# VectorE's dependent chains stood in pieces between the one-hot compares of a graph network's first aggregation

## The reference, cut to what matters

```
h = relu(layernorm(x))
norm = deg_inv[src] * deg_inv[dst]
m = norm * (h[dst] + (h[dst] * h[src]) @ W1.T + b)         # layer 0
x = x + leaky_relu(segment_sum(m, dst))
h = relu(layernorm(x))
h = relu(h @ Ws0.T + mean(h[src], dst) @ Wn0.T + c0)        # layer 1, two SAGE steps
h =      h @ Ws1.T + mean(h[src], dst) @ Wn1.T + c1
out = x + h
```

## Time and profile before

| | us |
|---|---|
| median of 3 runs | 3341.88 |
| lowest and highest | 3338.53, 3342.33 |
| profiled execution, its own time | 3346.14 |
| its span, first to last instruction | 3344.1 |
| aggregation 0 in it, slots 1 to 55 and the last products | 265 to about 1616 |

### The profile page before, as it was taken

One profiled execution on the slowest core, in us unless ns is written; L12 is line 12 of the kernel. 1 busy time (PEld: TensorE's weight loads), 2 busy tenths in 40 slices (PEclk: granted clock), 3 DMA queues, 4 the chain that ended last, 5 costly groups with the idle time before them and its releaser, 6 DMA issues.

```text
span 3344.1 us, 73461 instructions
## 1 busy us (share of the span) xinstructions
PE 2979.4 (89%) x27729; PEld 2602.2 (78%) x27729; DVE 1935.4 (58%) x5525; ACT 1322.4 (40%) x3331; POOL 2237.0 (67%) x2220
## 2 busy tenths in 40 slices
PE   1068788899998898989899999999999999999998
PEld 0046577688787787878788888888888888888888
DVE  6689999999898898989354444432221221222221
ACT  1324566687787787878244444421110000000000
POOL 7716765677777777777366665666664777677673
PEclk9999999999999999999999999999999999999999
DMA  7362344455455455545566666676665666666664
GB/s 213 96 123 79 105 121 120 125 152 158 140 164 151 139 151 164 158 138 150 160 202 221 219 196 212 219 238 195 215 201 166 215 221 219 209 209 211 215 216 153
DMA packets 479015, 581.78 MB, mean 174 GB/s; under 512 B 62620, under 2 KB 443265, under 8 KB 478169
## 3 DMA queue, kind: packets, MB, share of 16 engines
q1 hardware_dynamic: 352132, 404.43, 37.6%
q0 software_dynamic: 69168, 145.24, 16.6%
q10 hardware_dynamic: 57360, 27.34, 3.0%
HBM read 412.81 MB, written 164.77 MB: 173 GB/s over the span
## 4 chain that ended last, share of the span: by engine, by line
PE 59%; POOL 17%; DVE 16%; issue 7%; DMA 1%; ACT 1%; ACTq 0%; DVEq 0%; POOLq 0%
PE ps L1670 48%; POOL arena L1445 13%; DVE arena L1975 6%; DVE arena L1970 5%; PE ps L1581 4%; PE ps L1640 4%; POOL arena L1414 3%; PE ps L1616 2%; DMA arena<-parts,arena 1%; DVE arena L1989 1%; PE ps L1606 0%; POOL arena L1422 0%; DVE arena L2042 0%; DVE arena L2076 0%; DVE arena L2082 0%
## 5 line engine op out<-in xcount | busy, mean ns | idle before, releaser
L1445 POOL DMA_INDIRECT arena<-parts,arena x1991 | 2058.5, 1034 | 836.0 <-issue 573.1
L1670 PE MATMUL ps<-arena 128*128 128x256 f16 (+2 forms) x18816 | 2469.1, 274 | 65.1 <-DVEq L2043 58.0
L1670 PEld LDWEIGHTS ps<-arena 128*128 128x128 fp8e3 x18816 | 1805.2, 98 | 285.1 <-ACT arena L1237 59.6
L1237 ACT ACTIVATE arena<-ps 128x392 fp8e3<-128x392 f32 x2176 | 1048.9, 500 | 630.5 <-PE ps L1640 588.2
L1640 PE MATMUL ps<-arena 128*128 128x196 bf16 (+1 forms) x5806 | 786.7, 241 | 76.2 <-DVE arena L1975 66.5
L1640 PEld LDWEIGHTS ps<-arena 128*128 128x128 bf16 x5806 | 500.3, 101 | 189.5 <-DVE arena L1975 78.7
L1975 DVE TENSOR_TENSOR arena<-arena 128x1176 bf16<-128x1176 bf16 (+6 forms) x1016 | 644.7, 635 | 0.0
L1989 DVE TENSOR_TENSOR arena<-arena 128x256 bf16<-128x256 bf16 x864 | 232.7, 314 | 700.0 <-PE ps L1581 696.3
L1970 DVE TENSOR_TENSOR arena<-arena 128x768 bf16<-128x768 bf16 (+5 forms) x1016 | 539.8, 531 | 105.7 <-PE ps L1640 91.1
L1581 PE MATMUL ps<-arena 128*128 128x256 f16 (+1 forms) x1991 | 291.8, 275 | 39.4 <-DMA arena<-parts,arena 38.9
L2058 DVE SCALAR_TENSOR_TENSOR arena<-ps,rdegs,arena 128x128 f32<-128x128 f32 x196 | 68.6, 350 | 382.5 <-PE ps L1670 350.7
(11 more groups left out here) (192 smaller groups left out, 1142.1 us busy)
## 6 DMA issues: line engine op xcount, KB each, us to landing
arena<-counts SPq DMA_DIRECT2D x132, 1568.0 KB
counts<-arena SPq DMA_DIRECT2D x68, 1568.0 KB
arena<-parts,arena POOLq DMA_INDIRECT x1991
arena<-table SPq DMA_DIRECT2D x294, 64.0 KB
arena<-parts SPq DMA_DIRECT2D x28, 448.0 KB, 5.0
parts<-arena ACTq DMA_DIRECT2D x108, 64.0 KB
table<-arena ACTq DMA_DIRECT2D x108, 64.0 KB
parts<-arena SPq DMA_DIRECT2D x14, 455.0 KB, 9.5
```

Of the source, the lines that this page charges most:

```text
L1237: act.activation(to, ps[:, unit_bank(q), 0:(b - a) * tiles].rearrange("p (n a) -> p a n", n=b - a), ACT.Copy, saturate=False).then_inc(s_e ...
L1445: pool.indirect_dma_start(to, None, parts_of[nth], bass.IndirectOffsetOnAxis(ap=tail_idx[:, i, first + c:first + c + 1], axis=0)).then_inc ...
L1670: m = pe.matmul(bank(b, 0, w), stage[k][:, a, :], rows_in[nth][:, a, 0:w], start=e == 0, stop=e == tiles - 1, skip_group_check=True)
```

## The change

It touches aggregation 0 alone, on VectorE, and two places of small work on TensorE and ScalarE. `one_hots` is cut into `low_one_hots` and `high_one_hots`. `take` (for aggregation 0) is cut into `take_sum` and `take_rest`, `settle` into six functions of one instruction each, and `finish` into two. The loop issues one piece in front of a buffer's low compare and one between its low and high compare. A chain that started before buffer f is spread over f, f+1 and f+2. A piece waits for the last one by a semaphore as before (`link` only notes the value), but a compare stands between the two.

The sum of a dense tile (`take_sum`) is issued between the compares of the buffer before, so one high compare sooner, and `s_free` is raised by its second instruction itself. The check against the degree is now made last, from the copied sum in SBUF (130 columns are copied, not 129). `settle` begins at 0.20 and 0.58 of a slot and not at 0.22 and 0.66. TensorE's `w1_product` moves from product 60 to product 50, and ScalarE's two `turned_u` from 42 and 88 to 27 and 66 per cent of the slot.

```diff
-                take_before.setdefault(during(starts_at[g] + 1 if e else in_slot(s, 0.85)), []).append(2 * s + e)
-                settle_before.setdefault(during(in_slot(g, 0.66 if e else 0.22)), []).append(2 * s + e)
+                settle_before.setdefault(during(in_slot(g, 0.58 if e else 0.2)), []).append(2 * s + e)
+            tail_before.setdefault(during(in_slot(s, 0.85)), []).append(2 * s)
+            dense_before.setdefault(during(starts_at[g] + 1), []).append(2 * s + 1)
...
-                        now = [round(len(here) * part / 100) for part in (0, 8, 42, 46, 50, 54, 60, 88, 92, 96)]
+                        now = [round(len(here) * part / 100) for part in (0, 8, 27, 46, 50, 54, 60, 66, 92, 96)]
...
-                    if e == 60:
+                    if e == 50:
                         w1_product(nth, 2 * s)
...
+            def take_sum(j):
...
+                of = sums[:, r % SUMS, 0:width]
+                then(dve.tensor_scalar(of, bank(b, ONE, ONE + width), 1.0 / HIGH, None, ALU.mult))
+                dve.tensor_tensor(of[:, 0:ONE], bank(b, 0, ONE), of[:, 0:ONE], ALU.add).then_inc(free, 1)
+
+            def take_rest(j):
...
+                dve.tensor_tensor(u[:, e, :], tin[:, r % DEEP, :], of[:, 0:P], ALU.mult).then_inc(s_u, 1)
+                dve.tensor_tensor(s0b[:, t:t + 1], of[:, P:ONE], dinv[:, t:t + 1], ALU.mult)
+                if t < GROUPS:
+                    dve.scalar_tensor_tensor(agrees[:, t:t + 1], of[:, ONE:ONE + 1], HIGH, degree[:, t:t + 1], ALU.mult, ALU.is_equal)
...
+            def link(ins):
+
+                chain[0] += 1
+                ins.then_inc(s_chain, 1)
+                return chain[0]
...
+            def settle_leaky(j):
...
+                dve.wait_ge(s_chain, settled[0])
+                settled[0] = link(dve.scalar_tensor_tensor(v, v, SLOPE, v, ALU.mult, ALU.max))
...
+                    for j in dense_before.get(f, []):
+                        take_rest(j)
+                    for j in tail_before.get(f, []):
+                        take_sum(j)
                     for n in ready_before.get(f, []):
                         ready(0, n)
                     for j in settle_before.get(f, []):
-                        settle(j)
+                        settle_sum(j)
+                    for j in settle_before.get(f - 1, []):
+                        settle_leaky(j)
+                    for j in settle_before.get(f - 2, []):
+                        settle_stats(j)
                     for j in finish_before.get(f, []):
-                        finish(j)
+                        finish_root(j)
+                    low_one_hots(f)
+                    for j in tail_before.get(f, []):
+                        take_rest(j)
+                    for j in dense_before.get(f + 1, []):
+                        take_sum(j)
+                    for j in settle_before.get(f, []):
+                        settle_self(j)
+                    for j in settle_before.get(f - 1, []):
+                        settle_row(j)
+                    for j in settle_before.get(f - 2, []):
+                        settle_mean(j)
+                    for j in finish_before.get(f, []):
+                        finish_shift(j)
                         split_tile(0, j)
-                    one_hots(f)
+                    high_one_hots(f)
```

More of the change, by code:

```diff
@@ L2082, in settle, with settle_stats, settle_mean, finish_root @@
                 dve.scalar_tensor_tensor(x1[:, r % 3, :], v, 1.0 / (HIGH * BOTH), xin[:, r % DEEP, :], ALU.mult, ALU.add).then_inc(s_x1, 1)
+            def settle_stats(j):
+                r = at(0, j - 4)
+                if r is None:
+                    return
                 dve.wait_ge(s_x1, r + 1)
+                averaged[0] = link(dve.bn_stats(stats[:, r % 2, :], x1[:, r % 3, :]))
+            def settle_mean(j):
+                r = at(0, j - 4)
+                if r is None:
+                    return
+                dve.wait_ge(s_chain, averaged[0])
                 if r >= 2:
                     dve.wait_ge(s_std, r - 1)
-                then(dve.bn_stats(stats[:, e, :], x1[:, r % 3, :]))
-                dve.bn_aggr(tile_mv[:, e, :], stats[:, e, :]).then_inc(s_var, 1)
-            def finish(j):
+                dve.bn_aggr(tile_mv[:, r % 2, :], stats[:, r % 2, :]).then_inc(s_var, 1)
+            def finish_root(j):
                 r = at(0, j - 5)
@@ L2097, in finish, with finish_shift @@
                     dve.wait_ge(s_h, r - 1)
-                then(dve.reciprocal(tile_rstd[:, e:e + 1], tile_std[:, e:e + 1]))
+                rooted[0] = link(dve.reciprocal(tile_rstd[:, e:e + 1], tile_std[:, e:e + 1]))
+            def finish_shift(j):
+                r = at(0, j - 5)
+                if r is None:
+                    return
+                e = r % 2
+                dve.wait_ge(s_chain, rooted[0])
                 dve.scalar_tensor_tensor(tile_shift[:, e:e + 1], tile_mv[:, e, 0:1], -1.0, tile_rstd[:, e:e + 1], ALU.mult, ALU.mult).then_inc(s_shift, 1)
@@ L2142, in _ @@
                             dve.tensor_scalar(rdegs[:, k, :], rdeg[:, :], norms[:, 12 + k:13 + k], None, ALU.mult)
-                    for j in take_before.get(f, []):
-                        take(0, j)
+                    for j in dense_before.get(f, []):
+                        take_rest(j)
+                    for j in tail_before.get(f, []):
+                        take_sum(j)
                     for n in ready_before.get(f, []):
```

124 lines of the change are left out of this document (79 added, 45 removed).

## The result

| | us |
|---|---|
| before, median of 4 runs | 3341.8 (3338.5 to 3342.3) |
| after, median of 4 runs | 3382.2 (3380.8 to 3382.6) |
| ratio | 1.0122, 95% interval 1.0105 to 1.0140 |
| profiled execution after, its span | 3380.4 |

I had forecast 3314 us, in a range of 3290 to 3338. The change is slower, outside the range and on the other side.

What follows compares the result with a forecast made beforehand. VectorE was taken to bound 341 to 674 us and GpSimd's gathers 692 to 1568; links 22, `s_free` 3 and the later stretch 3 saved 28 us of 3346.1: 3318, or 3314 on the median's scale, range 3290 to 3338.

Steps and rivals of the forecast that it cites:

- the gathers' own duration: GpSimd's 597 gathers, 692 to 1568 us: lengthened by the compare running at their start; taken as 0, ends -22 and +31 us.
- The formula from the evenly spread starts: Mean gather excess if starts spread evenly over VectorE's compares, each costing up to its length less 0.13 us: 0.141 us; measured 0.178.
- One of my own signs of being wrong: The forecast is wrong if the mean gather differs from 1119 ns by more than 30 ns.
- The links: VectorE's chains before 674 us: seven links a tile lose their waits and overlap; 22 us, between 11.3 and 23.1.
- `s_free`: Signal to TensorE before 674 us comes about 0.9 us sooner, shortening its waits; 3 us, bounds 0 and 4.6.
- Granted clock above 0.97 in the first part: Sign in the changed profile: TensorE's granted clock above 0.97 from 341 to 674 us.
- Waits for one-hots and `s_free`: TensorE before 674 us: `s_free` waits near 0.8 us each or gone; growing one-hot waits would make the forecast wrong.
- The tie at 674 us: TensorE ends GpSimd's last long wait, 17.9 us, at 674, so VectorE's earlier savings move the whole rest forward.
- Gathers fall into step: Rival: each gather starts at a compare's beginning; decides from 47 ns a gather; at 80 ns 3362 us; chance 0.08.
- Links cost nothing: Rival: VectorE's pipe drain makes freed links worth nothing, leaving 3 + 3 us; 3336 us, chance 0.07.
- the Trainium skill's port rule: VectorE instructions with two SBUF inputs hold up GpSimd's SBUF reads; pieces count alike before and after, so no time.

Runs made afterwards that it cites:

- filled: joined with an unused, independent two-SBUF-input instruction between `settle_self` and `settle_leaky`, filling the idle moment; 3374.6 us, ratio 1.0103.
- joined: The change with `settle_leaky` moved right behind `settle_self`, so that it waits for its input again; 3312.5 us, ratio 0.9915.
- gapped: The change in its own order, but `settle_leaky` waits for the end of the high compare ahead of it; 3359.4 us, ratio 1.0049.
- the two light kernels: The kernel before and the change, each gathering at most 3 of up to 5 chunks a subgroup in aggregation 0; 3311.2 and 3262.2 us.
- after_again: The change, run again unaltered against the kernel before; 3382.9 us against 3342.5, ratio 1.0124.
- the ten orders: The kernel before, the change and eight follow-up kernels that rearrange sums, chain links, waits or added instructions, all gathers kept; 3312.5 to 3382.2 us.
- openings: The change with a one-column reciprocal ahead of three pieces of the `settle` chain; 3364.0 us, ratio 1.0071 to the kernel before.
- the ten streams: Kernel left out: 60 gathers each beside ten streams of VectorE instructions alone; mean gather 1195 ns with whole chains, 1518 with chains in pieces.

## Why the prediction was wrong

**The step that failed** is the one on the gathers' own duration: "What lengthens it is the compare that is running when it starts", and "The pieces change the spacing of the compares, not their number or length", from which I took 0 with ends of -22 and +31 us. In place of it: a gather can be passed over at the end of the running instruction, and then stands until VectorE is idle for a moment, or until its next instruction has at most one tensor input in SBUF (53 of the 55 held gathers came in ahead of such a one). The links' idle moments, which I counted as 11.3 us of waste, were such openings. filled against joined (one idle moment of 0.035 us a tile filled, 62 us lost, 12 held gathers to 49) is the strongest evidence, gapped against the change (23 us back, 55 held to 31) the second. The formula from the evenly spread starts could not hold this, since no term of it exceeds one instruction.

The size failed in two places. The 597 gathers that I had priced took 32.7 us longer, just past my end of 31. The 190 ahead of them I had not priced at all, since I took VectorE for the limit before 674 us and GpSimd's slack for cover; they took 36.7 us longer, used the slack up and made GpSimd the limit there too. The fifteenth transfer of counts starts 7.7 us later than before, where I had it 25 us sooner. From it to the last one the change loses another 30.6 us (949.1 against 918.5). One of my own signs of being wrong came true: the mean gather from 600 to 1450 us, 1119 ns before, is 1177, and I had allowed 30 ns.

The profile before had hints that I passed by. The longest gather there was 2447 ns, while a compare takes about 0.8 us at most, so one instruction could not explain it, and I had read the gathers' durations from 600 us on alone, which leaves out the one of 10.63 us at 346.89. And the excess, 178 ns, was above the 141 of my own formula; I read that as starts in step with the compares.

**The links** (22 us) **and `s_free`** (3 us) were right where the gathers have slack: 296.0 - 269.1 = 26.9 us for eleven slots in the two light kernels, where I had 25 for twelve. In the change itself this didn't come out: its 15th transfer of counts starts at 681.9 us, before it was 674.2, and TensorE waits for gathers from slot 5 on.

**"Granted clock above 0.97 in the first part"** was wrong: 0.94. TensorE stops for gathers instead. Waits for one-hots and `s_free` did shrink as told.

**The tie at 674 us.** I had GpSimd's 17.9 us wait move forward with TensorE. It shrank instead. GpSimd's waits, 341 to 692 us, in the change:

```profile
POOL arena L1423 <- PE ps L1550: 15.4, 2, 12.0
POOL arena L1446 <- PE ps L1582: 6.8, 5, 5.5
```

That was the slack that a longer gather eats first, before it costs anything; 56.0 us before and 22.2 now.

**The rivals.** "Gathers fall into step" had the right engine and the right sign: it decided from 47 ns a gather over the 597, and 55 came there (44 in after_again), with as much again ahead of them, where it counted nothing. I gave it 0.08 and 80 ns. Its picture (many starts at the beginning of a compare) was not what happened: from 692 to 1568 us the median gather got shorter. "Links cost nothing" fell: without the idle time the same work takes 27 us less. (It stands first in the list, not second. And I had set "VectorE: DVE Perf Modes" in the Trainium skill, section "The DRAIN you can't avoid", against the overlap without its exception: its first paragraph adds that a next instruction which is not held starts earlier. Rows 4, with 0.08 us of overlap, agree with that, so read whole the section did not put this part at nothing.) What I said of the Trainium skill's port rule, that it "gives no time of its own" since the pieces count before and after alike, was the same error: they count alike, but the moments between them don't.

**How far the explanation carries.** Over the ten orders with all gathers in place, time mostly follows the mean gather (ns, then us): 1119 (3312.5), 1123 (3318.2), 1131 (3328.2), 1134 (3341.8), 1160 (3364.0), 1169 (3347.1), 1186 (3359.4), 1213 (3374.6), 1227 (3382.2), 1228 (3381.1). Against a straight line through them (0.56 us a ns) openings is 18 us above and the kernel before 11 above, joined 10 below. Some 8 us of the first are lost before 350 us; the rest I have not traced. Open too is why a gather is passed over at one boundary and let in at another of the same kind.

The better version is joined: the change with one link moved, at 3312.5 us, 0.85% faster than the kernel before. It is 1.5 us from the forecast, but for a kernel that keeps an idle moment which the forecast counted as loss.

## What to carry to other kernels

Where GpSimd's gathers are near the limit, an idle moment of VectorE is not waste: it is where the gather gets in. Before packing two-input VectorE instructions back to back, look at the longest gather and at the maximum beside the median, and leave one dependent wait (0.035 us was enough here) in each run of them. Where the gathers have slack, packing pays: 49 us in the light kernels. When a few long gathers decide, a mean and an even-spread formula hide it; a maximum longer than any single instruction beside it says that the model is wrong.

## What the hardware showed that I had not expected

- A gather can be held over many instruction boundaries: 4.19 us behind ten VectorE instructions, 10.63 us behind 42 narrow compares in the kernel before, and 76.7 us beside a stream of two-input instructions with no gap.
- An idle moment of 0.035 us of VectorE behind the self link let in all 10 gathers that started 0.20 to 0.215 us into that link; without the moment 28 of 32 were held.
- Only that narrow range was at risk in this link: gathers that started up to 0.18 us into it, and those that started 0.22 us or more into it but before the next instruction, were not held.
- Two-input instructions with no gap don't always hold a gather: three of the ten streams were of this kind, and held none.
- VectorE instructions that don't wait for each other overlap by 0.07 to 0.09 us (L2120 ends at 394.67, L1980 starts at 394.60).
